# GpSimd copies for high parts, two low pieces behind each gather, and a last norm by pairs of tiles

## The reference

```
x = ln(x + dilated_attention(x))            # every other token of segments of 256, 16 heads
# top-1 mixture of 8 experts: y = (silu(x@w1[e])[:, :1024] * (x@w1[e])[:, 1024:]) @ w2[e], times max prob
x = ln(x + moe(x, router_w, router_b, w1, w2))
# linear attention: q, k = elu(..)+1; V = q (k^T v) / (q . sum k)
x = ln(x + linear_attention(x, W))
# soft mixture: logits = x.phi (64 x 32 slots); dispatch = softmax over the batch; combine = softmax over slots
#   slots = dispatch^T x;  y = slots @ W[n] + b[n];  out = combine @ y
x = ln(x + soft_moe(x, phi, W, b))
```

## Time and profile before

| | |
|---|---|
| median of 3 runs | 1475.33 us (1473.58 to 1475.54) |
| profiled execution | 1476.07 us |
| its span on the core | 1474.3 us |
| busy: TensorE | 1374.8 us, 93% |
| busy: VectorE | 894.3 us, 61% |
| busy: ScalarE | 658.5 us, 45% |
| busy: GpSimd | 794.2 us, 54% |

### The profile page before, as it was taken

The page is one execution under the profiler, slowest core; times in us unless marked ns, Lnnn a source line. Parts: engine busy times, 40 slices in busy tenths (PEclk is TensorE's granted clock), DMA queues, the critical chain, the costliest instruction groups (busy, mean ns, idle before and its releaser), DMA issues. The chain is left out here.

```text
span 1474.3 us, 29422 instructions
## 1 busy us (share of the span) xinstructions
PE 1374.8 (93%) x9361; PEld 1211.3 (82%) x9362; DVE 894.3 (61%) x1851; ACT 658.5 (45%) x1206; POOL 794.2 (54%) x694
## 2 busy tenths in 40 slices
PE   7996798999999995799988999999999998999997
PEld 3454687788888884677778999999999978999997
DVE  5778422232323332677578888888888864666655
ACT  4554333233333331666544444444444535555553
POOL 6663187777770002331039987987987957350400
PEclk9998799999999998899999999999999999999999
DMA  4112325222220002310032274574474487465450
GB/s 168 53 37 76 130 82 159 100 96 100 100 100 14 14 15 90 114 58 1 1 115 84 83 207 118 145 206 123 140 206 124 139 261 253 158 215 186 159 196 29
DMA packets 112526, 171.49 MB, mean 116 GB/s; under 512 B 6384, under 2 KB 97648, under 8 KB 106320
## 3 DMA queue, kind: packets, MB, share of 16 engines
q1 hardware_dynamic: 103440, 156.27, 33.1%
q0 software_dynamic: 3408, 9.31, 2.3%
q10 hardware_dynamic: 5616, 5.11, 1.0%
HBM read 115.22 MB, written 55.44 MB: 116 GB/s over the span
## 5 line engine op out<-in xcount | busy, mean ns | idle before, releaser
L2108 PE MATMUL comb_psO<-hand_parts,comb_eh 128*128 (+1 forms) x1024 | 197.8, 291 | 0.6 <-DVE hand_parts L1524 0.6
L1775 ACT ACTIVATE disp_raw<-disp_psL 128x512 f32<-128x512 f32 x128 | 76.6, 598 | 199.7 <-PE disp_psL L1687 113.6
L1088 DVE TENSOR_TENSOR moe_hs<-moe_psH,moe_act_a 128x512 f32<-128x512 f32 x78 | 50.3, 686 | 178.4 <-PE moe_psH L982 156.4
L2108 PEld LDWEIGHTS comb_psO<-hand_parts,comb_eh 128*128 128x128 f32 x1024 | 156.4, 189 | 1.1 <-issue 0.8
L1687 PE MATMUL disp_psL<-disp_ph,hand_xh 128*128 (+1 forms) x512 | 148.3, 290 | 0.8 <-DVE disp_e L1960 0.8
L1687 PE MATMUL disp_psL<-disp_ph,hand_xl 128*128 (+1 forms) x512 | 145.4, 284 | 0.0
L1687 PE MATMUL disp_psL<-disp_pl,hand_xh 128*128 (+1 forms) x512 | 145.4, 284 | 0.0
L2108 PE MATMUL comb_psO<-hand_parts,comb_el 128*128 (+1 forms) x512 | 143.7, 281 | 0.0
L2208 DVE TENSOR_TENSOR comb_el<-comb_psT,comb_eh 128x512 fp32r<-128x512 f32 x128 | 87.9, 688 | 88.0 <-ACT comb_eh L2142 84.5
L1711 PE MATMUL disp_psS<-disp_e,last_x 128*128 128x256 f32 x512 | 132.9, 382 | 4.3 <-POOL disp_e L1869 4.3
L982 PE MATMUL moe_psH<-w_hi,moe_xh 128*128 x312 | 128.0, 410 | 4.7 <-POOL w_lo L889 3.6
(11 more groups left out here) (287 smaller groups left out, 3962.4 us busy)
## 6 DMA issues: line engine op xcount, KB each, us to landing
logits<-disp_raw SPq DMA_DIRECT2D x64, 512.0 KB, 4.0
hand_e<-logits SPq DMA_DIRECT2D x32, 1024.0 KB, 6.6
w_raw<-in_w SPq DMA_DIRECT2D x8, 2048.0 KB, 7.8
disp_wt<-in_w_slot SPq DMA_DIRECT2D x16, 1024.0 KB, 10.0
w_raw<-in_w SPq DMA_DIRECT2D x8, 1024.0 KB, 10.5
slot_y<-disp_slots SPq DMA_DIRECT2D x64, 128.0 KB, 3.2
disp_bt<-in_b_slot SPq DMA_DIRECT2D x15, 512.0 KB, 4.9
comb_y_in<-slot_y SPq DMA_DIRECT2D x3, 2048.0 KB, 10.6
```

Of the source, the lines that this page charges most:

```text
L1088: v.tensor_tensor(hs[:, cols], psH[:, 2 + h, :], act_a[:, cols], ALU.mult).then_inc(hs_ready, 1)
L1775: nc.scalar.activation(raw[mc % 4][:, half * 2:half * 2 + 2, :], psL[l_bank[mc]][:, half * 2:half * 2 + 2, :], ACT.Copy).then_inc(copied, 1)
L2108: last = nc.tensor.matmul(psO[j % 2][:, 0:D], ep[s % EB][:, i, :], yp[:, bass.ds(odd, 1), ch * D:(ch + 1) * D].rearrange("p a d -> p (a d) ...
```

## The change

GpSimd's three sums with a column of zeros (L887, L1191, L2081) become `tensor_copy`; the column in `Weights` and its memset go. In the experts' GpSimd program no piece stands behind the gather of slot 3, and two pieces stand behind each gather from slot 4 on, until all 32 are issued (slots 4 to 19). In combine, VectorE's loop stops before the last batch, whose steps are written out; in them the norm of the tiles 4 and 5 is added from step 27 on (`pair_part(0, ...)`), one part a step, its last row behind the steps, and after the last tile only tiles 6 and 7 are normed (`pair_part(1, ...)`). SP stores the last half by two transfers of 256 KB, each when its pair is normed.

```
@@ Weights.divide
-            g.tensor_tensor(hi[:, e % 2, :], flat, self.zero[:].to_broadcast([P, flat.shape[1]]), ALU.add).then_inc(self.split, 1)
+            g.tensor_copy(hi[:, e % 2, :], flat).then_inc(self.split, 1)
@@ experts, gpsimd
+        AHEAD = 4
             for slot in range(FIRST_GATHERS, SLOTS):
                 gathers.issue(pool, slot)
-                if slot >= 3 and slot - 3 < w.LOW_CHUNKS:
-                    w.low_chunk(pool, 1, slot - 3)
-            nc.gpsimd.memset(w.zero[:], 0.0).then_inc(w.zeroed, 1)
-            pool.wait_ge(w.zeroed, 1)
+                if slot >= AHEAD:
+                    for n in range(2 * (slot - AHEAD), min(2 * (slot - AHEAD) + 2, w.LOW_CHUNKS)):
+                        w.low_chunk(pool, 1, n)
@@ linear_attention, gpsimd
-                nc.gpsimd.tensor_tensor(natural[:, t, :], x[:, t, :], zero[:].to_broadcast([P, D]), ALU.add)
+                nc.gpsimd.tensor_copy(natural[:, t, :], x[:, t, :])
@@ combine, sync
-            for h in (2 * B - 2, 2 * B - 1):
-                store(h)
-            sp.wait_ge(stored, 2 * B * 16)
+            store(2 * B - 2)
+            for w in (NT // 2 - 2, NT // 2 - 1):
+                sp.wait_ge(normed, 2 * w + 2)
+                sp.dma_start(dst[:, w, :, :], x[:, 2 * w:2 * w + 2, :]).then_inc(stored, 16)
+            sp.wait_ge(stored, (2 * B + 1) * 16)
@@ combine, gpsimd
-                    g_.tensor_tensor(yh[:, b % 2, cols], y_in[:, ch, :], zero[:].to_broadcast([P, D]), ALU.add).then_inc(y_split, 1)
+                    g_.tensor_copy(yh[:, b % 2, cols], y_in[:, ch, :]).then_inc(y_split, 1)
@@ combine, vector
+            LAST = B - 1
+
+            def pair_part(w, n):
+                cols, first = slice(2 * w, 2 * w + 2), HT + 2 * w
+                m, r, d, u = mean[:, cols], rstd[:, cols], var[:, cols], tmp[:, cols]
+                link = chained(LAST, 1 + w, 0 if n == 0 else START_LINKS + (n - 1) * NEWTON_LINKS)
+                if n == 0:
+                    wait(dve, stat, LAST * TB + first + 2)
+                    wait(dve, normed, LAST * TB + HT)
+                    norm_start(v, link, stats[:, first:first + 2, :], m, r, d, u, magic[:, cols])
+                elif n <= NEWTONS:
+                    norm_newton(v, link, r, d, u)
+                else:
+                    a = n - NEWTONS - 1
+                    v.tensor_scalar(row(LAST * TB + first + a), xo[:, first + a, :], m[:, a:a + 1], r[:, a:a + 1],
+                                    ALU.subtract, ALU.mult).then_inc(normed, 1)
+
+            PAIR_AT = STEPS - 1 - NEWTONS - 1
...
+                if last and s >= PAIR_AT:
+                    pair_part(0, s - PAIR_AT)
...
-            with dve.Fori(1, B) as b:
+            with dve.Fori(1, LAST) as b:
                 for s in range(STEPS):
                     step(b, s)
-            collect(B - 1, TB - 1)
-            for n in range(1 + NEWTONS + HT):
-                norm_part(B - 1, 1, n)
+            for s in range(STEPS):
+                step(LAST, s, last=True)
+            pair_part(0, NEWTONS + 2)
+            collect(LAST, TB - 1)
+            for n in range(1 + NEWTONS + 2):
+                pair_part(1, n)
```

## The result

The changed kernel takes 1467.68 us (median of 7 runs, 1462.39 to 1469.42), the kernel before 1475.33 beside it (7 runs, 1473.42 to 1477.34). The ratio is 0.9942, with an interval of 0.9932 to 0.9953: 7.65 us faster where 4.2 were forecast, inside the range of 1466.0 to 1475.5. The profiled execution took 1467.68 us, its span 1465.5.

What follows compares the result with a forecast made beforehand. TensorE, busy for 93% of the span, bounds the kernel, so GpSimd or VectorE edits pay only where it waits or after its last matmul. 2.6 + 0.3 + 1.35 = 4.25 us off gives 1471.1 beside 1475.33; range 1466.0 to 1475.5.

Steps and rivals of the forecast that it cites:

- The first stall: TensorE's 3.76 us wait at psY for low parts of expert 1's second weight; goes, as pieces end at 224.6 us.
- The hold: Gathers from slot 20 on wait for landings beside expert 2's weight load: a delay of 6 us, at least 4.2.
- the copy: GpSimd's copy of 4096 columns for expert 2 takes 3.65 us, where the sum took 7.02; low part ready at 267.0.
- B: Rival, chance 0.13: gathers land in under 5 us; expert 2's low part ready at 261.0, 13.5 us go, 1461.8 us.
- D: Rival, chance 0.07: gathers from slot 20 held 9.2 us per four; low part ready at 277.7, slower, 1481.8 us.
- Rival C: Chance 0.15: the copy is hardly cheaper than the sum, 7.0 us; low part ready at 270.4, total 1474.7 us.
- TensorE waits 6.1 us at psH: At expert 2's first weight TensorE arrives at 260.9 us and waits until the low part is ready at 267.0.
- The sum's term of 2.6 us: Expert 2's first low part is ready at 267.0 us instead of 269.6, so 2.6 us are gained there.
- Expert 3: TensorE's 0.3 us wait for expert 3's low part goes: ready at about 294 us, asked for at 298.6.
- the tail: Combine's end after TensorE's last matmul is 1.35 us shorter: 0.65 from two fewer rows, 0.7 from the last transfer.
- the cover: In combine, el's last piece ends at 1463.2 us, 0.9 us before TensorE needs it at 1464.1.
- Rival E: Chance 0.05: the cover fails or VectorE's last batch starts late in combine; 1.35 us are not gained, 1472.5 us.

Runs made afterwards that it cites:

- the kernel with the pause: Changed kernel with six serial memsets of 128x512 on GpSimd behind the gather of slot 32 only; 1468.52 us in one run.
- the one with fillers: Changed kernel with a memset of 128x512 behind each gather from slot 20 on; 1466.42 us in one run.
- the copies alone: Kernel before with only the three plain copies, the zero column still allocated; 1467.97 us, ratio 0.9949.
- the two experiments on it: Changed kernel with an unused column where the zero column stood, 1469.62 us; kernel before with its zero column behind the experts' buffers, 1472.14 us.
- the one with a spare column: Changed kernel with an unused column of 4 bytes where the zero column stood; 1469.62 us, ratio 0.9955.
- the one with the pieces alone: Kernel before with only the two low pieces behind each gather, sums kept; 1476.01 us, ratio 1.0009.
- the gathers late: Changed kernel with all 19 gathers of slots 20 to 38 in one row behind expert 3's division; 1459.82 us in one run.
- the spread kernel: Changed kernel with the gathers of slots 20 to 38 behind the divisions, four behind each expert's from expert 2 on; 1456.92 us, ratio 0.989.

## Why the prediction was right, and where it was lucky

**The first stall.** Right: pieces end at 224.75 (forecast 224.6), and no wait at psY for L874.

**The hold and the copy.** Right, rivals B and D are out: the gathers are held for landings three times. The hold was at the low end, though: the last gather starts 4.4 us later than 18 steps of 1.255 from 224.91 would put it (forecast 6, least 4.2). The other figures are near: division at 252.84 (254.3), copy 3.61 us (3.65), low part at 265.47 (267.0). Rival C is out. All three sizes measured here, 3.61 for 4096 columns, 1.91 for 2048 and 0.405 for 256 (in combine), lie within 0.04 us of the forecast's 0.15 us and 0.85 ns a column from two selects. The estimate of 6.1 us took the wrong one of two figures that "GPSIMD Engine Reference" of the Trainium skill, section 3.1, gives: not the 1.8 cycles an element but the 1.03 cycles for bodies bound by the ports, an estimate of 3.5 us at 1.2 GHz, agrees with the 3.61 measured.

**TensorE waits 6.1 us at psH.** This step failed. TensorE was to arrive at 260.9 and wait; it began slot 8's psH at 270.89, 5.4 us after the low part was ready, because it, ScalarE and VectorE stood still until 255. The size of the term came out right by luck, since two errors met: from the low part to slot 8's product are 11.36 us in the change, 8.27 in the kernel with the pause and 7.6 in the one with fillers. By these, one execution each, the standstill costs some 3.1 to 3.7 us beyond a plain wait, and 1.5 us came back from a division that was earlier than forecast. The statement that all of the first stall's gain is given back was right and even short: the copies alone reach slot 8 at 273.42, the whole change at 276.83.

**The sum's term of 2.6 us.** Before, the three tiles took 40.76 and now 38.33: 2.4. But the copies were worth 6.3 there by themselves, so in the whole change the pieces took back nearly 4. The change without the pieces (copies, pairs and the column gone) was not run. I had priced the two parts in a row, pieces first, and so did not see that with the first stall left in place the copy removes the second one whole.

**What the sum left out.** The removed column moved the experts' buffers by 32 bytes, and a tile takes 9.444 us instead of 9.527 (medians): 0.083 x 39 = 3.2 us, measured 2.8 and 2 in the two experiments on it. By the interval of the 2.8 (0.6 to 3.7) it is a part or nearly the whole of the difference between 4.2 forecast and 7.65. The column was in the diff, as one allocation that goes, and I had costed it at nothing without a word.

**Expert 3, the tail, the cover.** Right: no wait for expert 3's low part; the tail 1.43 us shorter (forecast 1.35), of it 0.65 from the rows (1.38 to 0.73) and 0.8 from the store (2.8 to 2.0). El's last piece ended at 1455.68. TensorE needed it two thirds through its 4.27 us, at 1456.7: a cover of 1.0 us (forecast 0.9). Rival E is out.

**The other copies** were free as forecast: 0.405 us each in combine instead of 0.617, and waited for by nobody.

## What to carry to other kernels

Price a step that is moved forward together with what then runs beside it: the gathers, pulled forward onto a 3 MB load, held each other, and what they brought cost as much as the stall they removed, and more than it beside the copies. The same gathers four at a time behind later work made the kernel 18 us faster than before (14 to 19 by the interval). When two stalls follow each other on one path, price each part of a change with the other part absent, too. When a diff drops or adds a buffer, list which addresses move.

## What the runs showed of the hardware

**A standstill of three engines beside a row of gathers.** In the changed kernel, the one with a spare column and the one with the pieces alone, all with gathers 1.25 us apart until 250 to 252 and no break after about 239, ScalarE and VectorE had gaps of up to 12.5 us. In all three the update of `a_ready` stands far behind the end of the matmul that makes it, 9.97 us in the changed kernel, 8.78 with the spare column and 9.92 with the pieces alone, and the engines go on 2.2 to 2.5 us after the last gather ends. In the kernels with fillers, with the gathers late and with them spread such updates come within 0.02 us. In the changed kernel and the one with the pieces alone, single sequencer instructions of TensorE also took about 0.7 us where they take 0.05 in the kernel with fillers. A gap of 0.54 us of memset behind each gather prevented the standstill, and one of 3.5 us interrupted it, in one execution each. So the density of the row at this place brings late signals. Why they are late is open: the same row 50 us later did nothing, and what differs there isn't known. One semaphore wait of TensorE's sequencer before psY (start, us, line), in the changed kernel and in the one with fillers:

```
247.21 0.70 Tensor EVENT_SEMAPHORE L1011
244.11 0.05 Tensor EVENT_SEMAPHORE L1016
```

The releasers "remote" and "issue" name no cause. Single updates are missing from the records: that of `a_ready` behind the matmul that ends at 226.13 in the changed kernel isn't there, and ScalarE's silu starts at 226.25 all the same. So a late update says something only where the waiting engine starts right behind it, as ScalarE does at 255.10.

**32 bytes.** A buffer's place at 32 beyond a multiple of 64 or on one changed the mean of the experts' matmuls psH from 399 to 391 ns and the median time of a tile from 9.527 to 9.444 us. The kernel's time moved by 2 to 3 us, one of the two comparisons being within its noise. Which of the moved buffers does it wasn't separated. The same shift made dispatch and combine no shorter.

**Landings.** A gather that lands in 2.8 us alone held the fourth after it by 2.83 us beside the weight load, which itself landed 12.0 us after its issue with four gathers beside it and 8.6 us after it with none, in the spread kernel.
